# Softmax shift in a cross-attention kernel: the row maximum split into two fp32r parts and added by one four-row product per bank

## The reference

```
x = x + xattn(layernorm(x), ctx, pos)
x = x + ffn(layernorm(x))

xattn: q = x @ Wq; k, v = split(ctx @ Wkv); 32 heads of 8
       q, k = rope(q, pos), rope(k, pos)
       w = softmax(q k^T / sqrt(8)) over 64 keys
       out = (w v) @ Wout + bout
ffn:   8 experts, the best 2 of each token, each
       (silu(x W1^T) * (x W2^T)) @ W3^T, weighted by a softmax of the two scores
```

## Time and profile before

| What | us |
|---|---|
| Runs | 573.99, 566.58, 574.38 |
| Median of the runs | 573.99 |
| Span of the profiled execution, first to last instruction | 570.8 |
| The profiled execution's own time | not recorded beside its span; the median run is 3.2 longer than the span |
| TensorE, busy in the span | 481.6 (84%) |
| VectorE, busy | 414.9 (73%) |
| ScalarE, busy | 326.3 (57%) |
| GpSimd, busy | 352.3 (62%) |

### The profile page before, as it was taken

One profiled execution on the slowest core, in us unless ns is written; L12 is line 12 of the kernel. 1 busy time (PEld: TensorE's weight loads), 2 busy tenths in 40 slices (PEclk: granted clock), 3 DMA queues, 4 the chain that ended last, 5 costly groups with the idle time before them and its releaser, 6 DMA issues.

```text
span 570.8 us, 21807 instructions
## 1 busy us (share of the span) xinstructions
PE 481.6 (84%) x7710; PEld 369.5 (65%) x7710; DVE 414.9 (73%) x1256; ACT 326.3 (57%) x849; POOL 352.3 (62%) x562
## 2 busy tenths in 40 slices
PE   2789999999999999999999877499999999999000
PEld 2556767676767676767675545279999999998000
DVE  6458898989998999999988757455555545554386
ACT  2375767677776767676767544256655655665000
POOL 5577688888888888888887532005555555555100
PEclk9999999999999999999999987579999999999555
DMA  5010322341222121212110104424333334331698
GB/s 109 28 28 22 118 71 66 107 133 47 75 59 79 55 70 37 71 37 70 37 42 24 59 21 139 111 66 133 118 123 121 120 122 129 117 113 67 200 378 305
DMA packets 55287, 54.61 MB, mean 96 GB/s; under 512 B 12933, under 2 KB 50959, under 8 KB 55184
## 3 DMA queue, kind: packets, MB, share of 16 engines
q1 hardware_dynamic: 43776, 31.69, 19.7%
q0 software_dynamic: 6480, 16.82, 7.9%
q10 hardware_dynamic: 4928, 4.72, 2.5%
HBM read 29.70 MB, written 23.90 MB: 94 GB/s over the span
## 4 chain that ended last, share of the span: by engine, by line
PE 59%; DVE 22%; issue 7%; DMA 5%; ACT 2%; POOL 2%; SPq 1%; DVEq 0%; POOLq 0%; ACTq 0%
PE logit_banks L1338 12%; DVE negmax L663 11%; PE logit_banks L1168 6%; PE logit_banks L1357 6%; PE bank L1208 6%; PE qkv_banks L1117 5%; PE logit_banks L1176 5%; DVE mid L648 4%; DMA mid<-result_rows 4%; PE qkv_banks L1108 3%; PE qkv_banks L1128 3%; PE bank L1316 3%; PE qkv_banks L1158 2%; PE qkv_banks L1347 1%; PE qkv_banks L1346 1%
## 5 line engine op out<-in xcount | busy, mean ns | idle before, releaser
L605 POOL DMA_INDIRECT result_rows<-w12a,blk_dest x71 | 69.4, 978 | 78.3 <-POOL blk_dest L598 44.4
L572 POOL DMA_INDIRECT routed_rows<-xs,slots x64 | 65.9, 1030 | 19.3 <-issue 16.8
L881 DVE TENSOR_TENSOR gated<-act_h,logit_banks 128x176 f32<-128x176 f32 x71 | 24.0, 338 | 71.5 <-ACT act_h L1068 65.4
L663 DVE TENSOR_REDUCE negmax<-logit_banks 128x16 f32<-128x1024 f32 x64 | 75.1, 1215 | 0.4 <-PE logit_banks L1149 0.4
L975 ACT ACTIVATE late<-logit_banks 128x1024 f32<-128x1024 f32 x64 | 62.0, 1021 | 17.2 <-PE logit_banks L1176 17.2
L579 POOL TENSOR_TENSOR mid<-rope_a,mid 128x512 f32<-128x512 f32 x32 | 41.0, 1283 | 29.6 <-DVE mid L648 29.6
L670 DVE RECIPROCAL rden<-bank 128x256 f32<-128x256 f32 x32 | 55.9, 1747 | 3.4 <-PE bank L1201 3.4
L1338 PE MATMUL logit_banks<-w_hi,x_hi 128*128 x142 | 47.9, 338 | 6.8 <-DVE x_lo L892 5.9
L1068 ACT ACTIVATE act_h<-logit_banks 128x176 f32<-128x176 f32 x71 | 22.5, 317 | 51.0 <-PE logit_banks L1338 51.0
L563 POOL TENSOR_TENSOR mid<-mid,mask 128x512 f32<-128x512 f32 x44 | 44.8, 1039 | 4.0 <-ACT mid L956 4.0
L1338 PE MATMUL logit_banks<-w_hi,x_lo 128*128 x142 | 46.6, 328 | 0.0
(11 more groups left out here) (185 smaller groups left out, 1333.0 us busy)
## 6 DMA issues: line engine op xcount, KB each, us to landing
xb<-routed_rows SPq DMA_DIRECT2D x71, 128.5 KB, 2.1
mid<-result_rows SPq DMA_DIRECT2D x32, 256.0 KB, 5.2
x_sb<-in_x_dram SPq DMA_DIRECT2D x32, 128.0 KB, 2.1
out_dram<-late ACTq DMA_DIRECT2D x16, 256.0 KB, 5.0
ctx_sb<-in_ctx_dram SPq DMA_DIRECT2D x32, 64.0 KB, 2.1
mid<-mT SPq DMA_DIRECT2D x128, 4.0 KB
w12a<-in_L_ffn_W_dram SPq DMA_DIRECT2D x2, 1024.0 KB, 6.6
routed_rows<-pad_row SPq DMA_DIRECT2D x11, 128.5 KB, 3.6
```

Of the source, the lines that this page charges most:

```text
L572: nc.gpsimd.indirect_dma_start(routed[:, :], bass.IndirectOffsetOnAxis(ap=slots[:, t.slot(TR), k:k + 1], axis=0), xs[:, t.slot(TR), k, :], ...
L605: nc.gpsimd.indirect_dma_start(results[:, :], bass.IndirectOffsetOnAxis(ap=blk_dest[:, b.slot(RB):b.slot(RB) + 1], axis=0), y_sb[:, b.slot ...
L663: V.tensor_reduce(negmax[:, t.par, 16 * half:16 * half + 16], ps_s[:, 1024 * half:1024 * half + 1024].rearrange("p (h k) -> p h k", k=N), ...
```

## The change

The maxima are split after the reduction by a new stage on VectorE, `split_peak`, which stands right behind `peak`: a copy of the 32 values to fp32r (rounded), and a subtraction which gives the exact rest, also fp32r. Each waits on a semaphore: the copy for the reductions, the subtraction for the copy. The transpose takes the 64 columns of both parts, and waits for the subtraction. ScalarE copies 64 partitions instead of 32. SyncE sends eight transfers per tile instead of four; afterwards each bank has four rows in `ms`: rounded part and rest, for each of the two halves of heads' queries, 512 values each. A constant `halves` [4 rows, 128] says which row goes to which half of the partitions. One fp32r product per bank, four rows deep, 128 partitions by 512 columns, takes the place of two fp32 products. `ms` is a buffer of its own, `xs` takes over the place of buffers of the opening, and the constants are set up by eight memsets of VectorE and two of GpSimd in place of one of VectorE.

```diff
-        mT = sb("mT", [HEADS, 2, P])
-        ones_row = sb("ones_row", [P, N])
+        split_max = sb("split_max", [P, 2, RG, 2, 8], FR)
+        mT = sb("mT", [2 * HEADS, 2, P])
+        ms = sb("ms", [P, 8 * N], FR)
+        halves = sb("halves", [P, P], FR)
...
                 for r in range(RG):
-                    sp.dma_start(ms[32 * r:32 * r + 1, :].rearrange("a (g n) -> a g n", n=P),
-                                 mT[8 * r:8 * r + 8, t.par, :]).then_inc(ms_in, 16)
+                    for c in range(2):
+                        row = 32 * r + 2 * c
+                        sp.dma_start(ms[row:row + 2, :].bitcast(F32).rearrange("s (g n) -> s g n", n=N),
+                                     mT[16 * r:16 * r + 16, t.par, N * c:N * c + N]).then_inc(ms_in, 16)
...
+            nc.gpsimd.memset(halves[:, 0:N].bitcast(F32), 0.0)
+            nc.gpsimd.memset(halves[:, N:P].bitcast(F32), 1.0).then_inc(pool_const, 1)
...
+            def split_peak(t):
+
+                dve.wait_ge(max_done, t.times(2, 2))
+                wait_past(dve, mT_done, t.n - 1)
+                whole = negmax[:, t.par, :].rearrange("p (r g) -> p r g", r=RG)
+                V.tensor_copy(split_max[:, t.par, :, 0, :], whole).then_inc(max_hi, 1)
+                dve.wait_ge(max_hi, t.n + 1)
+                V.tensor_tensor(split_max[:, t.par, :, 1, :], whole, split_max[:, t.par, :, 0, :].bitcast(F32),
+                                ALU.subtract).then_inc(max_lo, 1)
...
-            V.memset(ones_row[:], 1.0).then_inc(dve_const, 1)
...
+            for r in range(RG):
+                V.memset(halves[32 * r:32 * r + 2, 0:N].bitcast(F32), 1.0)
+                ins = V.memset(halves[32 * r:32 * r + 2, N:P].bitcast(F32), 0.0)
+            ins.then_inc(dve_const, 1)
...
                 do(peak, t.plus(1))
+                do(split_peak, t.plus(1))
                 do(best_scores, t.plus(-2))
...
-                pe.wait_ge(max_done, t.times(2, 2))
+                pe.wait_ge(max_lo, t.n + 1)
                 wait_past(pe, mT_sb, t.n)
-                M.transpose(ps_mT, negmax[:, t.par, :], ident[:]).then_inc(mT_done, 1)
+                M.transpose(ps_mT, split_max[:, t.par].rearrange("p r s g -> p (r s g)").bitcast(F32), ident[:])\
+                    .then_inc(mT_done, 1)
...
-                pe.wait_ge(ms_in, t.times(16 * RG, 16 * RG))
+                pe.wait_ge(ms_in, t.times(32 * RG, 32 * RG))
                 for r in range(RG):
-                    row = slice(32 * r, 32 * r + 1)
-                    for c in range(KC):
-                        ins = M.matmul(banks[r][64 * c:64 * c + 64, :], ones_row[row, :],
-                                       ms[row, :].rearrange("p (g c k) -> p g c k", c=KC, k=N)[:, :, c, :],
-                                       start=False, stop=True, skip_group_check=True)
+                    rows = slice(32 * r, 32 * r + 4)
+                    ins = M.matmul(banks[r], halves[rows, :], ms[rows, :], start=False, stop=True,
+                                   skip_group_check=True)
                     if r % 2:
                         ins.then_inc(st_done, 1)
```

More of the change, by code:

```diff
@@ L119, in xattn_ffn_kernel @@
         ps_q, ps_a, ps_rank = ps_qkv[:, 0:D], ps_qkv[:, D:D + E], ps_qkv[:, D + E:D + 2 * E]
-        ps_mT = ps_qkv[0:HEADS, D + 2 * E:D + 2 * E + P]
+        ps_mT = ps_qkv[0:2 * HEADS, D + 2 * E:D + 2 * E + P]
         ps_k, ps_v = ps_qkv[:, 512:768], ps_qkv[:, 768:1024]
@@ L138, in xattn_ffn_kernel @@
         negmax = sb("negmax", [P, 2, HEADS])
-        mT = sb("mT", [HEADS, 2, P])
-        ones_row = sb("ones_row", [P, N])
+        split_max = sb("split_max", [P, 2, RG, 2, 8], FR)
+        mT = sb("mT", [2 * HEADS, 2, P])
+        ms = sb("ms", [P, 8 * N], FR)
+        halves = sb("halves", [P, P], FR)
         rden = sb("rden", [P, D])
         attnT = sb("attnT", [P, D])
-        xs = sb("xs", [P, TR, 2, RW])
         gate_x = sb("gate_x", [P, TR + 1, E])
@@ L163, in xattn_ffn_kernel @@
         pos_sb = sb("pos_sb", [P, T, 2])
-        ang = sb("ang", [P, 2, T, 2, 2])
-        turns = sb("turns", [P, 2 * T * 4])
         cos_t = sb("cos_t", [P, T, 4])
@@ L173, in xattn_ffn_kernel @@
         pad_row = sb("pad_row", [P, RW])
-        wq_raw = sb("wq_raw", [P, KC, D])
-        wkv_raw = sb("wkv_raw", [P, 2 * D])
         wq_p = sb("wq_p", [P, KC, D + E])
@@ L216, in xattn_ffn_kernel, with first @@
         wtop = sb("wtop", [P, 2, T])
+        with ExitStack() as startup:
+            def first(name, shape):
+                return startup.enter_context(nc.sbuf_tensor(name, shape, F32))
+            wq_raw = first("wq_raw", [P, KC, D])
+            wkv_raw = first("wkv_raw", [P, 2 * D])
+            ang = first("ang", [P, 2, T, 2, 2])
+            turns = first("turns", [P, 2 * T * 4])
+        xs = sb("xs", [P, TR, 2, RW])
         with ExitStack() as attention:
@@ L234, in kqT @@
             return kqT_ring[t.slot(3)].rearrange("p (x n) -> p x n", x=4)
-        ms = mid[:, 2048:3072]
         rope_b, rot = mid[:, 3072:3584], mid[:, 3584:4096]
@@ L271, in xattn_ffn_kernel @@
             sem(s) for s in ("s_done", "max_done", "mT_done", "mT_sb", "ms_in", "st_done", "exp_done", "pv_done"))
+        max_hi, max_lo = sem("max_hi"), sem("max_lo")
         gate_x_done, gate_done = sem("gate_x_done"), sem("gate_done")
@@ L297, in xattn_ffn_kernel @@
         o_stored = [sem(f"o_stored{n}") for n in range(4)]
-        N_POOL_CONST, N_DVE_CONST, N_W = 9, 11, 2
+        N_POOL_CONST, N_DVE_CONST, N_W = 10, 11, 2
         NWT = 2 * E * KC + E
@@ L968, in copy_mT @@
                 act.wait_ge(mT_done, t.n + 1)
-                wait_past(act, ms_in, t.times(16 * RG, -16 * RG))
+                wait_past(act, ms_in, t.times(32 * RG, -32 * RG))
                 S.activation(mT[:, t.par, :], ps_mT, ACT.Copy).then_inc(mT_sb, 1)
```

## The result

| | Runs | Median us |
|---|---|---|
| Kernel before | 573.99, 566.58, 574.38, 567.33 | 570.66 |
| Changed kernel | 602.71, 604.25, 613.95, 604.43 | 604.34 |

A forecast was written before the change was run, and what follows sets the result against it. The hand-over order between TensorE and VectorE up to each tile's output product was taken as the bound. Tiles +2.8, startup +0.7 and ends +0.1 gave +3.6 us: 570.8 + 3.2 outside the span + 3.6 = 577.6, say 578; range 569 to 592.

The forecast's parts named there:

- two paths to the output product: Per tile, L1208 waits for TensorE's chain from the transpose and for VectorE's routing, reciprocal and L675; the later decides.
- the slack of half a microsecond on VectorE's path: Before the output product: L675 ends at 255.58, so its result is ready only 0.52 us before L1208 starts.
- one round of four: TensorE's addition of the maxima: four fp32r products run side by side in one round, taken as 0.236 us.
- the 0.38 that I took: TensorE, from L1168's stream to L1219: 0.62 us instead of 1.00, a gain of 0.38 us per tile.
- Rival (a): TensorE's four new products don't overlap or run at fp32 pace: 0.71 us more per tile, 600 us; chance 10%.
- rival (c): SyncE's eight transfers become the bound if each issue costs 1.0 us instead of 0.67: about 600 us; chance 5%.
- 0.44 with a bound of 0.50: VectorE's copy and subtraction let TensorE start the transpose L1158 0.44 us later per tile, bounds 0.38 and 0.50.
- on VectorE L702 and all to L675, also 0.45 later: VectorE behind the split: routing through L675 shifts by 0.45 us per tile, so L675 ends at 256.03.
- P: End of the second maximum reduction in a tile step, 252.67 before; the output product started 3.43 us after it.
- +0.09: Per-tile shift of output product L1208 by TensorE's path: 0.44 + 0.03 - 0.38 us; bounds about -0.07 and +0.36.
- Rival (b): VectorE's new steps collide with GpSimd's L537 or L551: slight form 583 us, 8%; full form 605 us, 6%.
- The opening: Startup on VectorE: eight small memsets enter, one leaves, +0.7 us on the chain, bounds 0 and 0.9.

The follow-up runs named there:

- the small delays: Kernel before plus one VectorE reduction of a constant behind `peak`, result unused, no split: 128x64 576.66 us (ratio 1.0068), 128x200 577.13 us (1.0083).
- the iota: Changed kernel with GpSimd's mask product replaced by an instruction that only writes the same buffer: 581.66 us, ratio to before 1.0167.
- 128x64 delay: Kernel before plus one VectorE reduction of 128x64 of a constant behind `peak`, result unused, no split: 576.66 us, ratio 1.0068.
- rounded maximum: Changed kernel without the split: the reduction writes the negated maximum rounded to fp32r, two-row products add it: 564.72 us, ratio to before 0.9833.

## Why the prediction was wrong

**What held.** The reading of the step and of its two paths to the output product held: the slack of half a microsecond on VectorE's path is what decided, and the small delays used it up as it said. The products: one round of four, starting almost together (0.51 us for all, 497 ns median each), and a gain of 0.42 where `chosen` is not in the way, near the 0.38 that I took. That the changed kernel shows 0.38 to the digit is luck, since L1243's weights waited for `chosen` there. Rival (a) is out. The eight transfers took 5.19 us of queue, ended at 261.52, put the load of x off to 261.63, and nobody waited for them; rival (c) is out. The split cost 0.49 us to L1183 (254.43 less 253.90, against 0.04 before), where I had 0.44 with a bound of 0.50.

**The step that failed** is the sentence "on VectorE L702 and all to L675, also 0.45 later". I moved these instructions as a rigid block. Of them `onehot` grew by 0.20 and `chosen` by 0.76, so that the attention was ready 4.36 after P (258.26) and not 3.36: the missing 1.00 is these two (0.96) and the split's few hundredths. With that in the sum, L1232 starts at 4.41 instead of 3.43, +0.98 per tile where I had +0.09, and 25 of the 31 steps measured 0.97 to 1.00. That 31 x 0.98 = 30.4 comes so near to the 30.2 of the span is chance: the other six steps, the opening and the end differ by more and by less.

**The rival that was nearest.** Rival (b) had the mechanism, and by luck even the time (605), but its instructions were wrong: it asked whether the copy and the subtraction collide with GpSimd. They didn't: 0.22 and 0.19. What collided were the instructions that they pushed. I held L710's 174 to 176 ns over 21 tiles against the rival; that row only says that L710 stood in a harmless place, in each tile the same one: beside two GpSimd instructions of 128x1 (one is L541 above), before the long ones begin. The row that mattered was in the timeline of the same step: L716 0.01 us ahead of L551, and L716's spread of 166 to 215. And before had the collision already, in a place where it cost nothing:

```profile
253.79 2.04 POOL L563 TENSOR_TENSOR mid<-mid,mask 128x512 f32<-128x512 f32 x2
...
255.57 0.28 DVE L723 TENSOR_TENSOR seen<-seen,chosen 128x8 bf16<-128x8 bf16 x1
```

`seen`, two inputs as well, ends 0.02 after the mask products do (255.85 at 255.83), and does so in each of the 21 tiles from 100 to 300 us, whatever its start, with 173 to 347 ns; in the changed kernel, clear of the mask product, it takes 152 in the median. The rule of the Trainium skill, "SBUF — State Buffer", section Who interferes with whom, which I had weighed in that rival, is borne out in the main: stretched to the end of GpSimd's instruction when that reads (0.97, 2.32), not when it only writes (0.17 beside the iota), not when VectorE has one input (0.17).

**The opening.** I had put +0.7 on it. The eight memsets are there, and the chain of waits shows their price up to TensorE's first product, 11.00 us instead of 10.11, 0.89 later. Behind that the chain runs over other work, and the first reduction starts at 25.66 us instead of 26.59, 0.93 earlier, not 0.7 later. In the profiles of the experiments it starts anywhere between 24.8 (128x64 delay) and 28.6 us (rounded maximum), so a term of 0.7 doesn't show in the end of the opening; what varies there I didn't test.

**Not settled.** When exactly GpSimd takes hold. `chosen` passed 0.10 us after the recorded start of L553, `onehot` 0.04 after it, while `chosen` 0.25 after was stopped; and 0.08 after the recorded start of the mask product, which follows L553 without a gap, it was stopped as well. A recorded start on GpSimd is thus not the moment from which VectorE is shut out; how long after it that is, why `seen` waited for both mask products though it started 0.21 before them, and why L710 before was not held beside L541, which reads SBUF too, stays open.

## What to carry to other kernels

Before an instruction is put into an engine's stream, look at what it pushes, not only at what it does: list, for each instruction behind it up to the next real wait, what the neighbour engine does at the place to which it moves. VectorE instructions with two inputs in SBUF beside long GpSimd instructions that read SBUF are a pair to list, however small the one on VectorE is; a form with one input takes it out of the pair. Where such a pair stands in the kernel already, the trace shows it: the short instruction ends with the long one in every tile, whatever its start. And where a constant shift is free to choose, as in a softmax, rounding it costs less than splitting it exactly.

## What the runs showed of the hardware that I had not expected

An addition of 128x8 took 0.97 us, to the end of one GpSimd instruction, and a bf16 one of the same size 2.32 us, to the end of two. The price of a delay in front of the first has a cliff: 0.28 us cost a step nothing, 0.49 cost it 0.94. And four fp32r products of four (or two) rows, 128 by 512, ran as one, 0.51 us from the first start to the last end; the engine's weight loads stood still for 0.39 us before theirs, which follow products of another shape.
